# A top-p search on rows with a long tail: from bisection to a guess and a narrower search

## Chip, cores and metric

The kernel runs on one core of a Trainium2 chip. The metric is the device time of one execution in microseconds (us). The kernel before takes 1705.38 us, the median of three runs (1704.26 to 1706.78).

## The reference

Two steps of a graph layer over N = 4096 nodes with 128 features. In each step `Xa` is mixed by an attention matrix of which every row keeps only its nucleus, and `Xf` by the normalised adjacency:

```python
R = (S + eye(N)); R = R / R.sum(-1, keepdims=True)
for n in range(2):
    q = Xa @ W1.T @ W2.T;  k = Xa @ W3.T
    probs = softmax(q @ k.T)                     # (4096, 4096)
    sp = sort_descending(probs);  cs = cumsum(sp)
    keep = (cs - sp) < 0.9                       # smallest set with 90% of the mass
    A = probs * keep;  A = A / A.sum(-1)
    Xf = R @ Xf;  Xa = A @ Xa
    Z = Z + Xf @ U1[n].T + Xa @ U2[n].T
out = layernorm(x + layernorm(x + Z) * ln_g + ln_b)
```

A row's nucleus is given by one number, the weight at which it is cut. The work of the change is to find that number for the rows in which it lies deep.

## The kernel before

Each step has three stages. The **ranking** goes over the 4096 rows in 8 blocks of 512: PE computes the logits, DVE takes the eight largest of each piece with MAX8, ACT exponentiates and sums them. From the sorted largest values (24 in step one, 64 in step two) DVE finds the cut of nearly every row (`stats_step`, L1585). `norm` and `top_exp` (the smallest sorted value that counts) are written to DRAM with the cut. A row whose cut lies below what was sorted is **hard**; POOL writes its number into a list. Meanwhile PE multiplies the adjacency for `Xf` (L873).

The **search** takes the hard rows 128 at a time, one row on each partition: a tile. POOL gathers the rows of x and their `href` (the cut so far, used as the exponent's offset) and `htop` by indirect DMAs; PE computes their 4096 logits, ACT exponentiates them into a 128x4096 array of weights. DVE then looks for the cut. `tile_begin` (L2064) sets up the target, 0.9 of the total. `halve` compares all weights with a trial value, sums those above it (two passes of 2048 in step two, `part_sum` L2085; one pass of 4096 in step one, L1862), and moves the trial (`next_try`). After four of these, `chord` interpolates a trial a little below the cut, one more sum checks it (`chord_step`, `settle_chord`), then the weights below the trial are written out and summed, their eight largest per 256 taken (MAX8, L1936 and L2163), 40 of them sorted in five rounds (`sort_round`), and the cut found among these (`tile_threshold`). `hflag` says whether a row was not settled by this; PE adds the flags over partitions (L1036, L1110), and if the sum is above zero a bisection of 23 sums runs over the whole tile (inside `dve.If`), which gives the cut in any case. The new cut and norm go back to DRAM by indirect DMAs.

The **mix** goes over 8 blocks of 512 columns with 16 units each. For a unit PE computes transposed logits minus the cut into one of three psL banks (L1125, L1126), ACT exponentiates (L1450), DVE zeroes what is below 1 (`mask`, L2257), PE multiplies the result with Xa (`weigh_unit`, L1138). PE weighs unit n-3 after the logits of unit n (LAG1 = 3), and there are three buffers before and three after the mask.

In step one the mix starts when the search is over. The loop runs once on this input, but it prepares the next tile's logits at its end. In step two the list has five tiles' fetches (the last is only prepared). Tile 0 is searched ahead of the mix, with PE idle. Tiles 1 to 3 are searched between the masks of pairs of blocks: tile p+1 in pair p (blocks 2p and 2p+1). The tables `FIRST_PAIR` and `WITHIN` (L2314 on) say which step of the search stands behind the mask of which unit k = 0 to 31 of the pair. Tile p+2 is prepared in pair p: transposed at unit 8, q at unit 9 (`tile_q_lo` on DVE), its logits behind the logits of units 10 to 13, `tile_begin` at unit 14. Two of its sums above a trial are made on ACT instead (`try_piece`, L1432: per trial four Relu and four Sign passes of 128x1024, at the units of `TRIED`), and read by DVE in `summed`; the fourth trial of `halve` starts at unit 31. All engines work through their instructions in the order written, with semaphores between them. `link` puts a wait for its own instruction behind a DVE instruction.

The adjacency loads of the last two parts of step one are on SP's queue behind the first gather; POOL adds the identity to one square of them (`add_self`, L608).

## Time and profile before

| | |
|---|---|
| median of three runs | 1705.38 us |
| profiled execution | 1707.06 us |
| its span | 1704.9 us |
| PE busy | 1536.4 us (90%) |
| DVE busy | 1319.2 us (77%) |
| ACT busy | 813.6 us (48%) |
| POOL busy | 235.6 us (14%) |
| mean granted clock of PE, share of full speed | 0.948 |

A number behind L is a line of the kernel. A row of the timeline gives the start in us from the start of the span, the duration in us, the engine, the line, the operation with out<-in, and in brackets how long the engine had been idle and what released it. `DVEq` is DVE's sequencer, which handles waits and semaphores. The span has the first step up to about 760 us, the second step's ranking up to 1184, the search of tile 0 up to 1241, the mix to 1683, and then the last rows and their store.

### The profile page before, as it was taken

How to read it: one execution, taken by the hardware profiler on the slowest of the kernel's cores; microseconds unless marked ns; L12 is line 12 of the kernel's file. 1: busy time of each engine (PE TensorE's matmuls, PEld its weight loads, DVE VectorE, ACT ScalarE, POOL GpSimd, SP SyncE). 2: the span in 40 equal slices, each digit the busy share in tenths (PEclk: the TensorE clock that was granted, in tenths of full speed). 3: DMA queues.
4: the chain of work that ended last, by engine and by line, in shares of the span. 5: the costliest groups of instructions: out<-in, count | busy, mean ns of one | idle time of the engine just before them, and what ended most of it. 6: DMA issues, size and time to landing. Idle time of an engine off the chain costs nothing. (4 is left out here: it accounts for less than half of the span.)

```text
span 1704.9 us, 18073 instructions
## 1 busy us (share of the span) xinstructions
PE 1536.4 (90%) x4753; PEld 886.7 (52%) x4753; DVE 1319.2 (77%) x3739; ACT 813.6 (48%) x1301; POOL 235.6 (14%) x272
## 2 busy tenths in 40 slices
PE   7999999877999999998999999995267988988996
PEld 4555556434555555554555656653134544544553
DVE  6788888656677777776899999998968788796554
ACT  4555555312555555564444444443122836734444
POOL 2010210212000000001011111122210211311322
PEclk9999999988999999999999999997578999998998
DMA  7466666462455555555566666670000000000000
GB/s 260 173 152 151 182 190 181 109 236 96 163 187 187 188 197 203 203 203 201 184 167 171 162 195 195 196 175 1 2 3 1 1 7 7 8 1 8 7 7 13
DMA packets 53084, 211.92 MB, mean 124 GB/s; under 512 B 22096, under 2 KB 30864, under 8 KB 32512
## 3 DMA queue, kind: packets, MB, share of 16 engines
q1 hardware_dynamic: 49728, 210.59, 39.6%
q0 software_dynamic: 3264, 0.30, 0.2%
q14 instruction: 59, 0.48, 0.1%
q8 instruction: 33, 0.54, 0.1%
HBM read 206.63 MB, written 4.48 MB: 124 GB/s over the span
## 5 line engine op out<-in xcount | busy, mean ns | idle before, releaser
L1272 ACT ACTIVATE psL<-psL,umax 128x1024 f32<-128x1024 f32 x256 | 278.5, 1088 | 296.2 <-DVE umax L1755 288.3
L1761 DVE MAX8 cand<-psL 128x8 f32<-128x256 f32 (+1 forms) x640 | 371.9, 583 | 56.9 <-PE psL L904 46.9
L903 PE MATMUL psL<-kA,mq 128*128 128x512 f32 x512 | 297.5, 581 | 3.0 <-ACT psL L1272 1.6
L873 PE MATMUL psO<-adj_in,xf 128*128 128x512 f32 x512 | 241.6, 596 | 4.9 <-POOL adj_in L608 4.9
L873 PE MATMUL psO<-adj_in,xn 128*128 128x512 f32 x512 | 242.5, 597 | 3.6 <-DMA adj_in<-in_adjT 1.9
L1084 PE MATMUL psO<-ebuf,xn 128*128 128x512 f32 x512 | 241.7, 593 | 0.0
L2028 DVE SCALAR_TENSOR_TENSOR ebuf<-ebuf 128x1024 f32<-128x1024 f32 x128 | 156.7, 1225 | 99.1 <-PE psO L1084 92.6
L904 PE MATMUL psL<-kB,mq 66*128 66x512 f32 x512 | 202.5, 395 | 0.0
L1450 ACT ACTIVATE ebuf<-psL 128x1024 f32<-128x1024 f32 x128 | 129.6, 1019 | 150.6 <-PE psL L1126 109.6
L1382 ACT ACTIVATE ebuf<-psL 128x1024 f32<-128x1024 f32 x128 | 131.0, 1023 | 134.2 <-PE psL L1053 134.2
L1138 PE MATMUL psO<-xf,xa 128*128 128x512 f32 x340 | 167.0, 615 | 12.4 <-DVE xf L2257 9.4
L1125 PE MATMUL psL<-mq,kA 128*128 128x512 f32 x256 | 150.2, 587 | 13.7 <-DVEq L2250 10.4
L1052 PE MATMUL psL<-mq,kA 128*128 (+1 forms) x256 | 148.2, 579 | 3.2 <-DVEq L1995 3.2
L2257 DVE SCALAR_TENSOR_TENSOR xf<-ebuf 128x1024 f32<-128x1024 f32 x85 | 105.8, 1248 | 55.8 <-PE psO L1138 34.8
L873 PEld LDWEIGHTS psO<-adj_in,xn 128*128 128x128 f32 x512 | 96.4, 191 | 79.4 <-issue 66.6
L873 PEld LDWEIGHTS psO<-adj_in,xf 128*128 128x128 f32 x512 | 95.8, 191 | 80.2 <-issue 71.7
L1084 PEld LDWEIGHTS psO<-ebuf,xn 128*128 128x128 f32 x512 | 96.7, 190 | 74.9 <-issue 64.3
L903 PEld LDWEIGHTS psL<-kA,mq 128*128 128x128 f32 x512 | 97.1, 190 | 73.8 <-issue 45.9
L904 PEld LDWEIGHTS psL<-kB,mq 66*128 66x128 f32 x512 | 97.1, 190 | 68.6 <-issue 56.8
L1126 PE MATMUL psL<-mq,kB 66*128 66x512 f32 x256 | 104.0, 406 | 0.0
L1053 PE MATMUL psL<-mq,kB 66*128 (+1 forms) x256 | 102.5, 400 | 0.0
L1138 PEld LDWEIGHTS psO<-xf,xa 128*128 128x128 f32 x340 | 64.9, 195 | 68.4 <-issue 48.2
(366 smaller groups left out, 2051.8 us busy)
## 6 DMA issues: line engine op xcount, KB each, us to landing
adj_in<-in_adjT SPq DMA_DIRECT2D x128, 1024.0 KB
adj_in<-in_adj SPq DMA_DIRECT2D x32, 2048.0 KB, 7.7
xaT<-in_xT SPq DMA_DIRECT2D x4, 512.0 KB, 5.3
xa_dram<-xa SPq DMA_DIRECT2D x8, 256.0 KB, 7.9
out<-t SPq DMA_DIRECT2D x8, 256.0 KB
list_dram<-ids,place POOLq DMA_INDIRECT x64
rel_prob<-cut_dram SPq DMA_DIRECT2D x32, 2.0 KB
cut_dram<-ncut SPq DMA_DIRECT2D x16, 2.0 KB
```

The source lines that it names most:

```text
L873: last = nc.tensor.matmul(psO[:], fs[:, j, :], adj_in[:, r % RING, j % JQ, :], start=(j == 0), stop=(j == JT - 1))
L903: nc.tensor.matmul(o, qA[:, t * P:(t + 1) * P], kA[:, c:c + BI], start=True, stop=False)
L904: last = nc.tensor.matmul(o, qB[0:DA + 2, t * P:(t + 1) * P], kB[0:DA + 2, c:c + BI], start=False, stop=True)
L1052: nc.tensor.matmul(o, kA[:, j * P:(j + 1) * P], mqA(i), start=True, stop=False)
L1084: last = nc.tensor.matmul(psO[:], xs[:, j, :], ekept[:, u % 2, hb * BI:(hb + 1) * BI], start=(j == 0), stop=(j == JT - 1))
L1125: nc.tensor.matmul(o, kA[:, j * P:(j + 1) * P], mqA(i), start=True, stop=False)
L1138: last = nc.tensor.matmul(psO[:], xs[:, j, :], kept_unit(n)[:, hb * BI:(hb + 1) * BI], start=(j == 0), stop=(j == JT - 1))
L1272: nc.scalar.activation(ps[:], ps[:], ACT.Exp, bias=umax[:, bass.ds(i * UB + k, 1)], scale=1.0, accum_out=usum[:, bass.ds(i * UB + k, 1)]). ...
L1382: nc.scalar.activation(eraw[:, u % 2, :], psL[buffer(u, MU)][:], ACT.Exp).then_inc(g["m_exp_done"], 1)
L1450: nc.scalar.activation(raw_unit(n), psL[w % 3][:], ACT.Exp).then_inc(g["slot_read"], 1)
L1761: last = v.max(cand[:, t % 2, at + c * 8:at + c * 8 + 8], psL[(turn + k) % 3][:, c * WIDE:(c + 1) * WIDE])
L2028: v.scalar_tensor_tensor(out=ekept[:, u % 2, :], in0=eraw[:, u % 2, :], scalar=1.0, in1=eraw[:, u % 2, :], op0=ALU.is_ge, op1=ALU.mult).th ...
```

## The change

Every hard row now also takes along the sum of its sorted weights. `norm` holds one over that sum (or over the kept part of it), so a third indirect gather fetches it (`hmass`, `hmasses`), and the ranking's statistics are changed so that for a hard row `norm` has the mass of all that `top_exp` bounds. A fill of `norm_dram[1]` with ones joins two others on SP.

`guess` takes the place of the set-up in `tile_begin`: it forms the mass outside the sorted elements, what share of it is to be dropped, and from a quadratic curve a first trial that lies some elements (25 in step one, 10 in step two) below the expected cut. Step one makes no sum above a trial: it goes from the guess straight to the weights below it. Step two makes two sums of the weights below the trial (`part_sum` with `is_lt`), each followed by `narrow`, which keeps the two ends of the interval and interpolates. `halve`, `chord`, `settle_chord` and the work on ACT are gone.

Step two sorts 48 in six rounds, not 40. The eight largest are taken from every 32nd group of eight weights, not every eighth group of 32 (the `k=32` views). A row whose trial fell on the wrong side of the cut now raises its flag as well, and the bisection starts from `tupper`. The tables are new: the search of a tile has steps 0 to 11 in place of 0 to 18, and of tile p+2 both sums are made in pair p at units 22 and 27.

The diff, cut to its core (the work on ACT, the ranking's other steps and the copies for step one's other names are left out):

```diff
-    FIRST = 4
-    NEXT = 40
-    BIAS = 10.0
+    NEXTS = [40] + [48] * (STEPS - 1)
+    AHEAD_OF = [(25.0,)] + [(10.0, 10.0, 22.0)] * (STEPS - 1)
...
-                    for dst in (ref_dram, top_dram[1]):
+                    for dst in (ref_dram, top_dram[1], norm_dram[1]):
...
-                    for dst, src in ((hrefs, ref_dram), (htops, top_dram[s])):
+                        pool.wait_ge(g["cut_late"], 48 + 64 * (NB - EARLY))
...
+                        nc.gpsimd.indirect_dma_start(
+                            out=hmass[:], out_offset=None, in_=norm_dram[s],
+                            in_offset=bass.IndirectOffsetOnAxis(ap=gid[:, 1:2], axis=0),
+                            bounds_check=N - 1, oob_is_err=False).then_inc(g["h_mass"], 16)
 
                     def kept_copies(n):
 
                         pool.wait_ge(g["h_x"], n * 48 + 48)
+                        pool.wait_ge(g["h_mass"], n * 16 + 16)
                         pool.sem_inc(met, 1)
                         link(nc.gpsimd.tensor_copy(gid_out[:], gid[:]))
                         link(nc.gpsimd.tensor_copy(htop_out[:], htop[:]))
+                        link(nc.gpsimd.tensor_copy(hmass_out[:], hmass[:]))
...
-                        pool.wait_ge(g["h_ref"], r * (PT * 32) + (c + 1) * 32)
+                        fetched = c + 2 if c < PT else c + 1
+                        pool.wait_ge(g["h_ref"], r * (PT * 48) + fetched * 48)
...
+            def share(out):
+
+                link(v.scalar_tensor_tensor(out=out, in0=hthird[:], scalar=1 / 3, in1=hthird[:], op0=ALU.add, op1=ALU.mult))
+
+            def guess(st, sums, top_, mass, ref, number):
+
+                here = slice(st, st + 1)
+                link(v.tensor_reduce(ttotal[:, here], sums, AX.X, ALU.add))
+                v.tensor_scalar(ttarget[:, here], ttotal[:, here], TOP_P, None, ALU.mult)
+                v.tensor_scalar(tupper[:, here], top_, 1.0001, None, ALU.mult)
+                v.tensor_scalar(tround[:, st, 0:1], ref, 2.0 ** -22, None, ALU.mult)
+                link(v.reciprocal(hin[:], mass))
+                link(v.scalar_tensor_tensor(out=hout[:], in0=ttotal[:, here], scalar=hin[:], in1=tupper[:, here],
+                                            op0=ALU.subtract, op1=ALU.add))
+                v.tensor_scalar(tround[:, st, 1:2], tround[:, st, 0:1], -1.0, None, ALU.mult)
+                link(v.tensor_scalar(hout[:], hout[:], 1e-20, None, ALU.max))
+                v.tensor_scalar(haim[:], ttotal[:, here], 1.0 - TOP_P, None, ALU.mult)
+                v.tensor_scalar(tunit[:, here], tupper[:, here], 1.5, None, ALU.mult)
+                link(v.reciprocal(tinv[:, here], hout[:]))
+                v.tensor_tensor(tround[:, st, 0:1], tround[:, st, 0:1], tround[:, st, 1:2], ALU.max)
+                v.tensor_copy(tnumber[:, here], number)
+                link(v.tensor_scalar(tgoal[:, here], haim[:], tinv[:, here], 1.0, ALU.mult, ALU.min))
+                v.tensor_scalar(telem[:, here], tupper[:, here], tinv[:, here], None, ALU.mult)
+                link(v.tensor_scalar(hthird[:], tgoal[:, here], 2 / 3, None, ALU.mult))
+                link(v.scalar_tensor_tensor(out=hguess[:], in0=hthird[:], scalar=1 / 3, in1=tgoal[:, here], op0=ALU.add, op1=ALU.mult))
+                v.tensor_scalar(tround[:, st, 0:1], tround[:, st, 0:1], -1.0, 1.0 - 2.0 ** -20, ALU.mult, ALU.add)
+                link(v.tensor_scalar(hguess[:], hguess[:], telem[:, here], AHEAD_OF[s][0], ALU.mult, ALU.mult))
+                link(v.tensor_tensor(hguess[:], hguess[:], tgoal[:, here], ALU.add))
+                link(v.tensor_scalar(hthird[:], hguess[:], 1.0, 2 / 3, ALU.min, ALU.mult))
+                share(tnow[:, st, 0:1])
+                link(v.tensor_scalar(ttry[:, here], tnow[:, st, 0:1], tunit[:, here], None, ALU.mult))
+
+            def narrow(st, e):
+
+                here, now = slice(st, st + 1), tnow[:, st, :]
+                link(v.scalar_tensor_tensor(out=haim[:], in0=hpart[:, 0:1], scalar=hpart[:, 1:2], in1=tinv[:, here],
+                                            op0=ALU.add, op1=ALU.mult))
+                v.tensor_scalar(hin[:], haim[:], tgoal[:, here], None, ALU.is_ge)
+                link(v.tensor_scalar(hthird[:], haim[:], 1.0, 2 / 3, ALU.min, ALU.mult))
+                v.tensor_scalar(hout[:], haim[:], tgoal[:, here], None if e > 0 else 2 / 3, *((ALU.is_lt,) if e > 0 else (ALU.is_lt, ALU.mult)))
+                share(tnow[:, st, 1:2])
+                if e == 0:
+                    v.tensor_scalar(thigh[:, st, :], now, hin[:], hout[:], ALU.mult, ALU.add)
+                    link(v.tensor_scalar(tlow[:, st, :], now, hout[:], 1.5, ALU.mult, ALU.mult))
+                else:
+                    v.tensor_tensor(hfrom[:], now, thigh[:, st, :], ALU.subtract)
+                    link(v.tensor_tensor(hto[:], now, tlow[:, st, :], ALU.subtract))
+                    v.scalar_tensor_tensor(out=thigh[:, st, :], in0=hfrom[:], scalar=hin[:], in1=thigh[:, st, :], op0=ALU.mult, op1=ALU.add)
+                    link(v.scalar_tensor_tensor(out=tlow[:, st, :], in0=hto[:], scalar=hout[:], in1=tlow[:, st, :], op0=ALU.mult, op1=ALU.add))
+                v.tensor_scalar(haim[:], telem[:, here], thigh[:, st, 0:1], 1.5 * AHEAD_OF[s][e + 1], ALU.mult, ALU.mult)
+                link(v.tensor_tensor(hspan[:], thigh[:, st, :], tlow[:, st, :], ALU.subtract))
+                v.tensor_tensor(haim[:], haim[:], tgoal[:, here], ALU.add)
+                link(v.tensor_scalar(hslope[:], hspan[:, 1:2], 1e-12, None, ALU.max))
+                v.tensor_scalar(hthird[:], haim[:], 1.0, 2 / 3, ALU.min, ALU.mult)
+                link(v.reciprocal(hslope[:], hslope[:]))
+                share(hguess[:])
+                link(v.tensor_scalar(hguess[:], hguess[:], tlow[:, st, 1:2], hslope[:], ALU.subtract, ALU.mult))
+                link(v.tensor_scalar(hguess[:], hguess[:], 1.0, hspan[:, 0:1], ALU.min, ALU.mult))
+                v.tensor_tensor(tnow[:, st, 0:1], hguess[:], tlow[:, st, 0:1], ALU.add)
+                link(v.scalar_tensor_tensor(out=ttry[:, here], in0=hguess[:], scalar=tlow[:, st, 0:1], in1=tunit[:, here],
+                                            op0=ALU.add, op1=ALU.mult))
...
                     if n == 0:
+                        return v.scalar_tensor_tensor(out=ncut[:, bass.ds(i * TB, TB)], in0=half[:], scalar=0.5, in1=mx[:],
+                                                      op0=ALU.mult, op1=ALU.subtract)
+                    if n == 1:
                         dve.wait_ge(g["st_ehalf"], i + 1)
-                        return v.scalar_tensor_tensor(out=half[:], in0=hard[:], scalar=-1.0, in1=half[:], op0=ALU.add, op1=ALU.mult)
-                    if n == 1:
-                        return v.tensor_tensor(ncut[:, bass.ds(i * TB, TB)], half[:], mx[:], ALU.subtract)
+                        return v.tensor_tensor(norm[:, bass.ds(i * TB, TB)], ehalf[:], kept[:], ALU.mult)
...
-                        for k in range(1, FIRST + 1):
-                            halve(weights, rest, k)
-                        chord()
-                        above(weights, rest)
-                        settle_chord()
+                        guess(0, hsum[:, bass.ds(turn, 1), :].rearrange("p o u -> p (o u)"), htop_out[:], hmass_out[:], href_out[:], gid_out[:, 0:1])
                         below(weights, rest)
...
+                        link(v.scalar_tensor_tensor(out=hflag[:], in0=htarget2[:], scalar=0.0, in1=hflag[:],
+                                                    op0=ALU.is_le, op1=ALU.max))
+                        v.scalar_tensor_tensor(out=hflag[:], in0=tnumber[:, 0:1], scalar=float(N), in1=hflag[:],
                                                op0=ALU.is_lt, op1=ALU.mult).then_inc(g["h_flag"], 1)
...
-                        if n < 2 * FIRST:
-                            halve(c, 1 + n // 2, n % 2)
+                        if n < 4:
+                            part_sum(c, n % 2, ALU.is_lt)
+                            if n % 2 == 1:
+                                narrow(tile_slot(c), n // 2)
+                        if n in (4, 6):
+                            part_sum(c, (n - 4) // 2, ALU.is_lt)
+                        if n in (5, 7):
+                            part_largest((n - 5) // 2)
                         if n == 8:
-                            chord(c)
-                        if n in (9, 10):
-                            chord_step(c, n - 9)
-                        if n in (11, 13):
-                            part_sum(c, (n - 11) // 2, ALU.is_lt)
-                        if n in (12, 14):
-                            part_largest((n - 12) // 2)
-                        if n == 15:
                             tile_sort(c)
                             for m in range(3):
                                 sort_round(m)
-                        if n == 16:
+                        if n == 9:
                             for m in range(3, NEXT // 8):
                                 sort_round(m)
-                        if n == 17:
+                        if n == 10:
                             tile_threshold(c)
-                        if n == 18:
+                        if n == 11:
                             tile_settle(r, c)
 
-                    FIRST_PAIR = {k: k for k in range(18)}
-                    FIRST_PAIR[19] = 18
-                    WITHIN = {0: 5, 1: 6, 3: 7, 4: 8, 5: 9, 6: 10, 9: 11, 10: 12, 12: 13, 14: 14, 16: 15, 17: 16, 18: 17, 19: 18}
-                    BEGIN_AT, SUMMED_AT, FOURTH_AT = 14, (21, 30), 31
+                    FIRST_PAIR = {0: 0, 2: 1, 4: 2, 6: 3, 8: 4, 9: 5, 11: 6, 12: 7, 14: 8, 16: 9, 18: 10, 19: 11}
+                    ONE_AHEAD = {22: 0, 27: 1}
+                    WITHIN = {0: 2, 2: 3, 5: 4, 6: 5, 8: 6, 10: 7, 13: 8, 15: 9, 17: 10, 19: 11}
+                    BEGIN_AT = 14
...
-                                if k in SUMMED_AT:
-                                    summed(r, p + 2, 1 + SUMMED_AT.index(k))
-                                if k == FOURTH_AT:
-                                    search_step(r, p + 2, 4)
+                                if k in ONE_AHEAD:
+                                    search_step(r, p + 2, ONE_AHEAD[k])
...
-                    for n in range(19):
+                    for n in range(12):
                         search_step(0, 0, n)
-                        if n == 2:
+                        if n == 1:
                             z_rows(NB - 1, 0)
-                        if n == 5:
+                        if n == 3:
                             z_rows(NB - 1, 1)
-                        if n == 12:
+                        if n == 8:
                             tile_q_lo(0, 1)
```

## Rows read from the trace of the kernel before

**Rows 1.** The page, chain that ended last, shares of the span by line.

```profile
...
PE psO L1138 9%; DVE xf L2085 3%; PE psL L1125 2%; PE psL L1126 2%; DVE xf L2257 2%; DVE cand L2163 1%; DVE ebuf L2257 1%; ACT dropped L1432 0%; PE psT L1146 0%; ACT ebuf L1450 0%; DVE parts L2263 0%; ACT t L1466 0%; PE psT L1117 0%; DVE mq L2247 0%; DMA norm_dram<-hnorms,gids 0%
```

**Rows 2.** Busy time by stretch, blocks 0 to 6 of the mix: stretch, length, then each engine.

```profile
...
1252.60:1326.60 74.00, 55.78 (x156) 31.01 (x154) 63.75 (x122) 26.33 (x35) 0.07 (x1) 0.89 0.00 0
1326.60:1372.70 46.10, 43.13 (x131) 24.58 (x130) 34.44 (x80) 36.93 (x56) 12.33 (x11) 0.95 0.03 7
1372.70:1435.10 62.40, 54.42 (x167) 31.38 (x166) 52.85 (x111) 26.00 (x39) 11.90 (x10) 0.95 0.01 1
1435.10:1486.80 51.70, 45.51 (x139) 25.90 (x138) 37.07 (x95) 40.07 (x61) 12.93 (x9) 0.93 0.04 11
1486.80:1542.30 55.50, 48.15 (x139) 25.10 (x137) 51.29 (x99) 19.86 (x26) 10.19 (x7) 0.97 0.01 3
1542.30:1594.10 51.80, 45.93 (x134) 26.26 (x135) 32.82 (x80) 22.95 (x31) 13.40 (x10) 0.90 0.02 4
1594.10:1638.30 44.20, 44.20 (x139) 25.41 (x139) 26.47 (x41) 20.47 (x27) 14.06 (x10) 1.00 0.03 7
```

**Rows 3.** Timeline of DVE, search of step one.

```profile
...
361.52 4.49 DVE L1862 SCALAR_TENSOR_TENSOR ebuf<-xa,htry 128x4096 f32<-128x4096 f32 x1
...
366.75 4.49 DVE L1862 SCALAR_TENSOR_TENSOR ebuf<-xa,htry 128x4096 f32<-128x4096 f32 x1
...
406.56 0.28 DVE L1836 TENSOR_TENSOR mq<-psT,mq 64x128 fp32r<-64x128 f32 x1
...
407.62 0.16 DVE L1968 CAST hflags<-psT 128x1 int32<-128x1 f32 x1 [0.52 <-DVEq L1534]
```

**Rows 4.** Timeline of PE, the same stretch.

```profile
...
373.66 27.63 PE L873 MATMUL psO<-adj_in,xn 128*128 128x512 f32 x64
...
404.00 0.33 PE L1004 MATMUL psT<-ident,xg 128*128 128x128 f32 x1 [1.31 <-DMA htop<-top_dram,gid]
...
406.89 0.59 PE L1036 MATMUL psT<-hflag,ones 128*128 128x1 f32 x2 [1.73 <-DVE mq L1836]
```

**Rows 5.** Timeline of POOL, the two additions of the identity in that stretch.

```profile
...
359.39 1.68 POOL L608 TENSOR_TENSOR adj_in<-adj_in,ident 128x128 f32<-128x128 f32 x4 [9.01 <-DMA adj_in<-in_adjT]
392.68 3.69 POOL L608 TENSOR_TENSOR adj_in<-adj_in,ident 128x128 f32<-128x128 f32 x4 [31.61 <-DMA adj_in<-in_adjT]
```

**Rows 6.** Timeline of DVE, search of tile 0 in step two.

```profile
...
1184.38 0.16 DVE L2068 TENSOR_REDUCE ttotal<-hsum 128x1 f32<-128x4 f32 x1 [0.17 <-DVEq L1534]
...
1185.77 2.35 DVE L2085 SCALAR_TENSOR_TENSOR xf<-adj_in,ttry 128x2048 f32<-128x2048 f32 x1
...
1218.65 2.35 DVE L2085 SCALAR_TENSOR_TENSOR xf<-adj_in,ttry 128x2048 f32<-128x2048 f32 x1
...
1236.70 0.16 DVE L2215 CAST hflags<-psT 128x1 int32<-128x1 f32 x1 [0.34 <-DVEq L1534]
...
1247.93 0.42 DVE L2246 CAST cuth<-rel_prob 2x512 fp32r<-2x512 f32 x1 [3.86 <-DMA cum_keep<-cut_dram]
```

**Rows 7.** Timeline of PE, the same stretch.

```profile
...
1224.22 0.77 PE L960 MATMUL psL<-kA,hq 128*128 128x512 f32 x1 [16.01 <-DVE hq L1736]
...
1229.70 0.39 PE L961 MATMUL psL<-kB,hq 66*128 66x512 f32 x1
1235.97 0.59 PE L1110 MATMUL psT<-hflag,ones 128*128 128x1 f32 x2 [5.88 <-DVEq L2201]
```

**Rows 8.** Timeline of DVE, block 0 of the mix.

```profile
...
1285.70 1.23 DVE L2257 SCALAR_TENSOR_TENSOR xf<-ebuf 128x1024 f32<-128x1024 f32 x1 [0.22 <-DVE ttry L2107]
...
1289.68 1.23 DVE L2257 SCALAR_TENSOR_TENSOR ebuf<-ebuf 128x1024 f32<-128x1024 f32 x1 [0.22 <-DVE ttry L2142]
...
1296.74 1.22 DVE L2257 SCALAR_TENSOR_TENSOR xf<-ebuf 128x1024 f32<-128x1024 f32 x1 [3.38 <-PE psO L1138]
...
1322.36 1.23 DVE L2257 SCALAR_TENSOR_TENSOR ebuf<-ebuf 128x1024 f32<-128x1024 f32 x1 [1.94 <-ACT ebuf L1450]
```

**Rows 9.** Groups by line and shape, DVE, 1240 to 1600 us: busy us, mean ns.

```profile
...
L2163 DVE MAX8 cand<-xf 128x8 f32<-128x256 f32 x48 | 16.2, 408 | 0.0
```

More of the change, by code:

```diff
@@ L84, in gnn_kernel @@
     LOWEST = -1e30
+    LEAST = 1e-30
     PAIRS = NB // 2
@@ L317, in step_sems @@
             if s == 0:
-                names += ["h_l", "h_exp", "h_done", "m_l_ps", "m_exp_done"]
+                names += ["h_l", "h_exp", "h_done", "h_mass", "m_l_ps", "m_exp_done"]
                 names += ["r_n_ps", "r_n_sb", "m_n_ps", "m_y_sb", "m_yt_ps", "m_yt_sb", "xa_out"]
@@ L577, in _ @@
             link(nc.gpsimd.memset(htops[:], 1.0))
+            link(nc.gpsimd.memset(hmass[:], 1.0))
+            link(nc.gpsimd.memset(hmasses[:], 1.0))
             for p in range(PAIRS):
@@ L1261, in stats_half @@
                     nc.scalar.activation(top_exp[:, i * TB:(i + 1) * TB], top_rel[:], ACT.Exp)
-                    nc.scalar.activation(ehalf[:], half[:], ACT.Exp).then_inc(g["st_ehalf"], 1)
+                    nc.scalar.activation(ehalf[:], half[:], ACT.Exp, scale=-0.5).then_inc(g["st_ehalf"], 1)
                 def rank_block(i, prev, more, turn):
@@ L1652, in cut_step @@
                     if n == 14:
-                        return v.tensor_tensor(keep[:], rel[:], bc(low[:], TOP), ALU.is_ge)
+                        return v.tensor_tensor(keep[:], rel[:], bc(top_rel[:], TOP), ALU.is_ge)
                     if n == 15:
```

247 lines of the change are left out of this document (59 added, 188 removed).

## The prediction

> **What bounds the kernel now.** I read the page's chain first. The reader is to see that it follows the mix of step two: PE's weighing (L1138) leads it, and DVE's sums above a trial (L2085) come second with 3% of the span, ahead of the masks [rows 1]. Then the stretches of the mix, block by block. Block 6, in which nothing is searched, takes 44.2 us with PE busy throughout; that is the floor. Blocks 0 to 5 take 74.0, 46.1, 62.4, 51.7, 55.5 and 51.8, together 341.5, where six floors are 265. In blocks 0, 2 and 4 DVE is busy for 63.8, 52.9 and 51.3 us, more than PE has work for; there DVE sets the pace, and in block 1 it is busy for 34.4 of 46.1 and does not [rows 2]. Third, DVE's timelines of the two searches that stand ahead of a mix. In step one the search begins at 361.5, but its flag is read at 407.62 [rows 3], and PE is busy with the adjacency until 401.3 (373.66 + 27.63) [rows 4]: this search is nearly hidden. In step two tile 0 is searched from 1184.38 to 1236.70 with nothing beside it [rows 6]; PE has only the next tile's logits there [rows 7].
>
> **Step one.** Four halvings, the chord and its check go, five sums at 5.23 us each (366.75 - 361.52) [rows 3]. The search then ends near 383, and that gains almost nothing, since PE reaches the flag only after the adjacency. What is left is the order on DVE: `prepare` stood behind the search and ran at 406.56, a microsecond after q was there. Now DVE waits for it, so q's low part is done at 405.8 and not 406.84: 1.0 gained [rows 3]. What is late next is POOL's gather, which landed at 404.0; PE had been idle for 1.31 us by then, of which ACT's copy of its last transposes explains about 0.7 and the gather 0.6 [rows 4]. It was issued behind an addition of the identity that took 3.69 us beside DVE's search; the same work took 1.68 with DVE idle [rows 5]. DVE will be idle, so the gather comes 2 us earlier and PE starts at 403.4: 0.6 more. The third gather is behind the two that PE waits for and ends (some 1.3 us later) before POOL needs it; the copy of `hmass` costs 0.2 on the way to `h_done`. One instruction less in the tail of each ranking gives 0.2 in each step. SP's fill stands behind its last load, under 40 us of adjacency work, so nothing; uncovered it would be 0.4. Together -1.0 - 0.6 + 0.2 - 0.2 = -1.6, bounds 0 and -3.
>
> On the addition of the identity, the Trainium skill (SBUF — State Buffer, Who interferes with whom) says that a DVE instruction with two SBUF inputs and a GpSimd instruction that reads SBUF take one port in turn, and the second waits. By that rule 3.69 becomes 1.68; without it the gather stays late and the sum would be 0.6 smaller.
>
> **Tile 0 of step two, exposed.** From the set-up to the first sum below the trial it now takes 34.3 us (1218.65 - 1184.38) [rows 6]. After the change: the guess, two sums of two passes, two `narrow`, and the two `z_rows` (1.1 us) that stay. A pass is 2.35 and 2.4 with the read of the accumulator [rows 6]: 9.6. The trace does not have the new chains of small instructions. The nearest is the chord, 15 instructions, 11 of them linked: between two masks 3.98 us apart it takes 2.8 (mask 1.14 to the next start) [rows 8], some 0.24 per linked one. The guess has 13 linked (3.4 with its operands that are pointers), `narrow` 11 and 12 (3.3 and 3.5). As bounds I take 0.16, the busy time of one [rows 6], and 0.35 per linked one. Sum 3.4 + 9.6 + 6.8 + 1.1 = 20.9, so 13.4 less. Against it: a sixth round of sorting (0.7), 48 in place of 40 elements and one more flag instruction (0.3). DVE's flag is then ready at 1223.6. But PE has tile 1's logits in front of the flag. They wait for `tile_q_lo`, which DVE issues behind the first three rounds, at about 1218.5, and took 5.9 us with PE at its lower clock (1224.22 to 1230.1) [rows 7]. PE comes to the flag at 1224.8, not 1235.97. So the gain is 11.2, not 12.4. Everything behind it (value load, hcut, scatter, loads of the cut) moves as one. The guess for tile 1 is 2 us longer than its set-up, but DVE waited 3.86 us for the cut behind it [rows 6]: hidden.
>
> On the small instructions, the Trainium skill (VectorE: DVE Perf Modes, The TRN2 errata) has a table by which a DVE instruction on SBUF costs 58 cycles plus its elements at 0.96 GHz, 61 ns for one element. The trace has 160 ns [rows 6], and I go by that; by the page's figure the new chains would be a third as long and the whole change some 15 us better.
>
> **The mix.** Sums above or below a trial fall from 28 passes to 18, each 2.5 us between masks. I take the blocks one by one; all of it is DVE time, which counts in full where DVE sets the pace.
> - Block 0: 12 passes become 6 (-15.4), four `next_try` (-3.6), chord (-2.8), settling (-0.9); two `narrow` (+6.8), longer guess (+2.0). The mask that waited 1.94 for ACT, whose next exponential stood behind a try waiting for the set-up, doesn't wait now [rows 8]. The stall of 3.38 at unit 10 stays: PE's tile logits wait for `tile_q_lo` of a DVE that is late. Masks that stand alone pay a handshake each, +1. Net -15, 59 us.
> - Block 1: both sums of tile 2 come in, at units 6 and 11. One pass and one `narrow` more, and a slot of 9.3 us with `cut_rows`, against 3 us of `summed` that go. DVE has 11.7 us of room [rows 2], but the slot is longer than the three buffers cover (about 7 us): +2.
> - Block 2: three passes go (-7.6), tails and chord (-5.5), the wait for ACT (-1.9); one `narrow` (+3.5), guess (+2.0), six rounds of sorting moved in (+5.0): -4.5.
> - Block 3: those rounds are gone from it (-4.3), `summed` (-3), a pass and a `narrow` come (+5.9) where there is room: -3.
> - Blocks 4 and 5: as 2 and 3 without a guess or a tile ahead: -4.6 and -3.5.
> Sum -28.6. ACT loses some 38 us of tries, none of which was on the path beyond the waits named. POOL's third gather per tile (1.3 us) lies 30 us ahead of its use. At the end the set-up of a fifth tile is 2 us longer, behind which only the last store is waited for, and that is longer: nothing.
>
> MAX8 now reads groups of eight 32 groups apart. The trace shows only groups of 32, at 408 ns each as recorded, 0.34 apart [rows 9]. Per tile that is 5.4 us. I take no change; if it took twice as long, 5 us more in each of the four tiles of step two.
>
> **The sum.** -1.6 - 0.2 (step two's ranking) - 11.2 - 28.6 = -41.6 on the profiled execution's 1707.1 (span 1704.9 and 2.2 around it), 1665.5. That execution is 1.7 above the median of the runs, so 1663.8.
>
> **Rivals.**
> 1. *The guess misses (ends slower).* Step one makes no sum to check it: for each of up to 128 rows the trial must lie between 0 and 40 elements below the cut, 25 being aimed at. One row outside, or eight of the wanted ones in one of the 16 groups, raises the flag, and the bisection runs: 23 sums of 5.2 and one more, 125 us, at 407 where nothing covers it. 1663.8 + 125 = 1789. From the first such row it decides. In step two two sums correct the guess and 48 are sorted, so it is less likely; it would cost 135 per tile. For it: 128 rows with one curve for all. Against: one tile of at most 128 among 4096 rows lies past the 24 sorted, so most lie not far past them, and 15 to 25 elements is then a wide margin. No row of the trace bears on it, so the chance is a judgement.
> 2. *The bursts eat the gain.* Slots of 7 to 9 us among masks of 1.14 exceed the buffers; PE stands, and the idle slots behind cannot give it back. If blocks 1, 3 and 5 gain nothing and 0, 2 and 4 half, the mix gives 12: 1680.
> 3. *The mix goes to PE's floor.* If blocks 2 to 5 come within 2 us of 44 to 48, the mix gives 45: 1647.
> 4. *It is hidden anyway*, the loss of sums being taken up by the narrows, as DVE's sum of small instructions grows by 28 us. Then only tile 0 counts, 1694. Against: rows 2, DVE-bound blocks.
>
> **Chances.** The forecast 0.72, rival 1 0.12, rival 2 0.08, rival 3 0.06, rival 4 0.02. The range 1645 to 1683 holds the forecast with its bounds and rivals 2 and 3. 0.2% (3.4 us) is about what a measurement can tell from no change: faster 0.87, same 0.01, slower 0.12.
>
> **What would show it.** Step one: PE's flag at about 405, one sum of 4.49 in the search, no bisection. Tile 0: the flag is read near 1223.5 (1225.5 less the earlier gain), with PE's logits just before it. The mix: block 0 near 59, block 2 near 58, block 4 near 51, blocks 1, 3, 5 near 48; L2085 has 18 passes there. 400 to 408 ns for MAX8. Wrong would be a dozen or more sums of 4.49 in step one, or blocks 0, 2 and 4 above 65, 60 and 54.

## The result, and the profile after

The changed kernel takes 1677.52 us (median of 4 runs, 1671.42 to 1678.37) beside 1705.95 for the kernel before on the same chip: ratio 0.9827, interval 0.9802 to 0.9852. That is 28.4 us less, where 41.6 were forecast. The direction was right, and so was the mechanism for tile 0 and for blocks 0, 2 and 4. The mix gave 18 us and not 28.6: blocks 1 and 3 came out 12.5 us worse than forecast, and block 5 gave 4.8 of that back. The profiled execution took 1678.12 us (span 1676.3, before 1704.9).

The chain on the page still follows PE's weighing through the mix (L1148 is before's L1138); the sums above or below a trial (L2085 before, L2067 after) fell from 3% to 2%:

```profile
...
PE psO L1148 8%; PE psL L1135 2%; PE psL L1136 2%; DVE xf L2067 2%; DVE xf L2174 1%; DVE ebuf L2174 1%; DVE cand L2079 1%; ACT ebuf L1441 0%; PE psL L970 0%; PE psT L1156 0%; PE psL L971 0%; DVE parts L2180 0%; DVE cand L2094 0%; POOL rstd 
```

Busy time by stretch, blocks 0 to 6 of the mix, in the columns of [rows 2] (length, then PE, weight load, DVE, ACT, POOL, granted clock, DMA):

```profile
...
1241.60:1301.98 60.38, 51.14 (x151) 29.86 (x149) 51.25 (x123) 22.90 (x28) 1.78 (x2) 0.91 0.00 1
1301.98:1358.17 56.19, 48.11 (x133) 27.02 (x134) 39.62 (x92) 22.53 (x29) 14.46 (x10) 0.88 0.01 1
1358.17:1417.80 59.63, 54.86 (x171) 31.63 (x169) 50.67 (x129) 27.57 (x38) 17.18 (x11) 0.97 0.03 10
1417.80:1470.94 53.14, 46.49 (x130) 26.22 (x129) 38.06 (x85) 21.51 (x28) 14.85 (x9) 0.87 0.01 1
1470.94:1521.46 50.52, 47.87 (x147) 26.63 (x146) 47.05 (x106) 21.30 (x27) 9.50 (x7) 1.00 0.04 11
1521.46:1564.99 43.53, 42.51 (x134) 24.26 (x134) 29.56 (x63) 22.72 (x30) 14.06 (x10) 1.00 0.01 2
1564.99:1609.21 44.22, 44.22 (x139) 25.43 (x139) 26.47 (x41) 20.67 (x27) 15.06 (x11) 1.00 0.02 7
```

Beside [rows 2]: block 0 fell by 13.6, 2 by 2.8, 4 by 5.0, 5 by 8.3; block 1 rose by 10.1 and block 3 by 1.4. In blocks 1 and 3 DVE is busy for 39.6 of 56.2 and 38.1 of 53.1 us, so neither engine fills them, and the granted clock is at its lowest of the mix. Block 7 begins at 1609.21, before at 1638.30: 29.1, all of the gain.

Groups of DVE from 1240 to 1600 us, where before there were 28 of these sums at 2345 ns:

```profile
...
L2067 DVE SCALAR_TENSOR_TENSOR xf<-adj_in,ttry 128x2048 f32<-128x2048 f32 x18 | 44.2, 2458 | 0.0
L2079 DVE MAX8 cand<-xf 128x8 f32<-128x256 f32 x48 | 16.2, 407 | 0.0
```

Timelines of DVE, then PE and POOL, in step one; they answer to [rows 3 to 5]:

```profile
...
361.21 0.16 DVE L1534 TENSOR_REDUCE ttotal<-hsum 128x1 f32 x1 [8.32 <-ACT xa L1368]
...
364.64 4.49 DVE L1898 SCALAR_TENSOR_TENSOR ebuf<-xa,ttry 128x4096 f32<-128x4096 f32 x1
...
380.92 0.16 DVE L1955 SCALAR_TENSOR_TENSOR hflag<-tnumber,hflag 128x1 f32<-128x1 f32 x1
405.75 0.28 DVE L1885 TENSOR_TENSOR mq<-psT,mq 64x128 fp32r<-64x128 f32 x1 [24.66 <-ACT mq L1360]
```

```profile
...
374.34 27.63 PE L883 MATMUL psO<-adj_in,xn 128*128 128x512 f32 x64
...
404.24 0.32 PE L1014 MATMUL psT<-ident,xg 128*128 128x128 f32 x1 [0.88 <-ACT xf L1237]
```

```profile
...
393.21 1.69 POOL L610 TENSOR_TENSOR adj_in<-adj_in,ident 128x128 f32<-128x128 f32 x4 [31.21 <-DMA adj_in<-in_adjT]
```

One sum, no bisection; q's low part at 405.75 (406.56 before); PE waits for ACT's copy and no longer for the gather. Tile 0 of step two, DVE and then PE, beside [rows 6, 7]:

```profile
...
1183.24 0.16 DVE L1534 TENSOR_REDUCE ttotal<-hsum 128x1 f32<-128x4 f32 x1 [0.17 <-DVEq L1522]
...
1205.13 2.34 DVE L2067 SCALAR_TENSOR_TENSOR xf<-adj_in,ttry 128x2048 f32<-128x2048 f32 x1
...
1223.09 0.16 DVE L2116 SCALAR_TENSOR_TENSOR hflag<-tnumber,hflag 128x1 f32<-128x1 f32 x1
...
1225.89 0.16 DVE L2132 CAST hflags<-psT 128x1 int32<-128x1 f32 x1 [2.13 <-DVEq L1522]
1229.79 0.16 DVE L2150 RECIPROCAL hkept<-hkept 128x1 f32<-128x1 f32 x1 [3.75 <-remote]
```

```profile
...
1218.66 0.77 PE L970 MATMUL psL<-kA,hq 128*128 128x512 f32 x1 [10.08 <-DVE hq L1785]
...
1225.47 0.28 PE L1120 MATMUL psT<-hflag,ones 128*128 128x1 f32 x2
```

And block 1, the two places at which PE stands longest, PE first, then DVE's work behind unit 11. A slot is the time from the start of one unit's mask to the start of the next:

```profile
...
1310.50 0.50 PE L1120 MATMUL psT<-hflag,ones 128*128 128x1 f32 x2 [3.67 <-DVEq L2118]
...
1350.37 3.78 PE L1148 MATMUL psO<-xf,xa 128*128 128x512 f32 x4 [4.28 <-DVE xf L2174]
...
1355.37 1.88 PE L1148 MATMUL psO<-xf,xa 128*128 128x512 f32 x4
```

```profile
...
1337.72 1.51 DVE L2174 SCALAR_TENSOR_TENSOR ebuf<-ebuf 128x1024 f32<-128x1024 f32 x1 [2.77 <-ACT ebuf L1441]
1339.16 3.35 DVE L2067 SCALAR_TENSOR_TENSOR xf<-adj_in,ttry 128x2048 f32<-128x2048 f32 x1
...
1342.56 1.11 DVE L1562 SCALAR_TENSOR_TENSOR haim<-hpart,tinv 128x1 f32<-128x1 f32 x1
...
1346.78 0.68 DVE L2156 TENSOR_TENSOR mq<-psT,mq 64x512 fp32r<-64x512 f32 x1
...
1349.09 2.36 DVE L2174 SCALAR_TENSOR_TENSOR xf<-ebuf 128x1024 f32<-128x1024 f32 x2 [0.41 <-DVE mq L2164]
```

From the mask at 1337.72 to the next at 1349.09 are 11.4 us: this is the long slot. PE runs out of masked units, stands for 4.28, and what follows runs at 1.2 GHz: four weighing matmuls take 3.78 us there and 1.88 five us later. In the kernel before, the longest stop of blocks 1 and 3 was another one, early in block 3, and ACT ended it:

```profile
...
1443.05 3.78 PE L1138 MATMUL psO<-ebuf,xa 128*128 128x512 f32 x4 [6.19 <-ACT oT L1454]
...
```

ACT was at work there on the tries that the change removes. After the change no stop of PE over 0.9 us in these blocks ends with ACT. That the tries made it late is not shown by a run.

### The profile page after: what moved, and what is told of

It reads as the page before. It is cut to its first block and busy times, and to the rows that moved or that the text cites. A ratio compares the mean times of both kernels' runs of the same rounds, so it can differ in the third digit from the quotient of the medians.

```text
span 1676.3 us, 17981 instructions
## 1 busy us (share of the span) xinstructions
PE 1535.3 (92%) x4753; PEld 889.1 (53%) x4753; DVE 1267.7 (76%) x3735; ACT 779.8 (47%) x1237; POOL 245.6 (15%) x283
## 5 line engine op out<-in xcount | busy, mean ns | idle before, releaser
L1148 PE MATMUL psO<-xf,xa 128*128 128x512 f32 x340 | 167.9, 617 | 5.8 <-DVE xf L2174 5.6
L1135 PE MATMUL psL<-mq,kA 128*128 128x512 f32 x256 | 152.9, 597 | 11.2 <-DVEq L2167 11.2
L1148 PEld LDWEIGHTS psO<-xf,xa 128*128 128x128 f32 x340 | 66.5, 198 | 60.6 <-issue 45.4
```

The lines of the kernel that those rows point to most:

```text
L1135: nc.tensor.matmul(o, kA[:, j * P:(j + 1) * P], mqA(i), start=True, stop=False)
L1148: last = nc.tensor.matmul(psO[:], xs[:, j, :], kept_unit(n)[:, hb * BI:(hb + 1) * BI], start=(j == 0), stop=(j == JT - 1))
```

## The experiments

All edits are on the changed kernel. The kernel before was timed again beside each group of experiments (e1 to e4, e5 to e8, e9 to e11, e12), and its median lay between 1705.95 and 1708.94 us. So each ratio is to the kernel before as timed beside it; the changed kernel's is 0.9827. Four experiments leave the mix as it is (e4, e7, e8 and e9). With the changed kernel they show how far an unchanged mix varies: blocks 0 to 5 take 323.4 us in the changed kernel and 320.9, 323.3, 324.6 and 320.0 in the four, block 1 54.4 to 56.2, block 3 50.8 to 53.1. Part of that is the granted clock behind one and the same stop: PE stands for 3.7 us at the flag of block 1 in all of them, and over the 8 us behind it the clock is 0.57 in the changed kernel and 0.79 in e7 and e9.

**e1, the long slot.**

```diff
-                    ONE_AHEAD = {22: 0, 27: 1}
+                    ONE_AHEAD = {22: 0, 30: 1}
```

> Edit: in blocks 1 and 3 the second sum ahead and its narrow stand behind unit 14 (k = 30), not behind unit 11, where q's low part and cut_rows stand too. Theory A (one slot is too long): the slot of 11.4 us falls to about 4.2, PE's idle time of 4.28 us behind it goes in both blocks with the stretch at the lower clock that follows it; blocks 1 and 3 fall from 56.2 and 53.1 us to about 50 and 48, the time by 8 to 12 us, to about 1667. Theory B (only the sum of DVE's work in a block counts, wherever it stands): the blocks stay within 1 us, the time within 2 us of the changed kernel. Theory C: unit 14 is as bad a place, since normed_spread stands behind unit 13 and block 2's burst comes after; then 0 to 4 us.

1670.55 us, ratio 0.9776 (0.9758 to 0.9794), 7 us below e4, which was timed beside it. Blocks 1 and 3:

```profile
...
1300.91:1353.51 52.60, 48.21 (x140) 27.32 (x140) 38.82 (x93) 23.44 (x30) 14.77 (x12) 0.94 0.02 6
...
1413.12:1462.69 49.57, 46.64 (x137) 26.46 (x135) 37.27 (x85) 22.41 (x29) 12.90 (x9) 0.93 0.03 7
```

Theory A, somewhat smaller: PE stands nowhere for as much as 0.9 us behind unit 11, with nearly the same work for DVE (38.8 and 37.3 us busy, for 39.6 and 38.1). POOL's last addition of a block's rows also fell from 3.20 us beside the sum to 1.33, and the sum from 3.35 to 2.34.

**e2, the flag.**

```diff
-                            if u == 3 and i % 2 == 1 and p < PT:
+                            if u == 4 and i % 2 == 1 and p < PT:
```

with ACT's `tile_cut` at u = 5 and DVE's settling (step 11) at k = 20.

> Edit: in odd blocks PE's flag matmul stands one unit later (u = 4), DVE's settling and ACT's logarithm of the cut too. Theory A: PE's idle time at the flag (3.67 us in block 1, 2.20 in block 3, 1.02 in block 5) is the lateness of a DVE whose threshold stands behind unit 1 or 2; one unit later DVE has caught up and 3 to 6 us go, mostly in block 1. Theory B: PE would only wait for the mask in place of the flag, since the same DVE is late for both; then within 1.5 us of the changed kernel.

1670.27 us (1669.34 to 1676.41), ratio 0.9780 (0.9758 to 0.9802), so the time alone says little. PE in block 1:

```profile
...
1314.74 0.38 PE L1120 MATMUL psT<-hflag,ones 128*128 128x1 f32 x2 [1.01 <-DVEq L2118]
1351.66 3.78 PE L1148 MATMUL psO<-xf,xa 128*128 128x512 f32 x4 [6.96 <-DVE xf L2174]
```

The wait at the flag fell from 3.67 to 1.01, and the one at the long slot rose from 4.28 to 6.96 by the same 2.7 us: a PE that is earlier stands longer where DVE is late. Blocks 0 to 5 took 316.2, 4 to 8 below an unchanged mix, and block 1 53.2, 1 to 3 below. Both theories hold in part.

**e3, nothing ahead.**

```diff
-                    ONE_AHEAD = {22: 0, 27: 1}
+                    ONE_AHEAD = {}
...
-                                within = FIRST_PAIR if p == 0 else WITHIN
+                                within = FIRST_PAIR
```

> Edit: nothing is summed ahead in blocks 1 and 3; tiles 2 and 3 are searched within blocks 2 and 4 from their first sum on, in the places that tile 1 has in block 0. Theory A (DVE sets the pace in even blocks, a long slot in odd ones): blocks 1 and 3 lose the first sum, the long slot and its stalls, 56.2 and 53.1 become about 48 and 45, while blocks 2 and 4 take two sums and two narrows more (about 16 us of DVE) and become like block 0 and worse, about 68 and 60; sum +2 to +6 us. Theory B (bursts cost nothing, work counts): +12 to +16 us.

1681.30 us, ratio 0.9840 (0.9822 to 0.9858). Blocks 1 to 4, then block 5's flag on PE:

```profile
...
1300.32:1350.16 49.84, 46.05 (x134) 26.37 (x135) 31.12 (x70) 22.78 (x30) 13.10 (x10) 0.93 0.01 1
1350.16:1413.58 63.42, 52.56 (x164) 30.52 (x163) 55.44 (x145) 26.21 (x37) 18.70 (x11) 0.95 0.03 9
1413.58:1460.18 46.60, 44.34 (x134) 25.47 (x135) 31.04 (x70) 22.61 (x30) 13.40 (x9) 0.96 0.01 1
1460.18:1518.60 58.42, 51.58 (x145) 28.07 (x144) 54.55 (x121) 20.65 (x27) 11.32 (x7) 0.91 0.02 6
```

```profile
...
1527.11 0.41 PE L1120 MATMUL psT<-hflag,ones 128*128 128x1 f32 x2 [3.66 <-DVEq L2118]
```

Theory A. In block 1 the two sums ahead cost 4.6 to 6.4 us, not the 2 net that I had for them; moving them into blocks 2 and 4 costs 2 to 4 and 8 there. Block 5 takes 48.2 for 43.5, which theory A had left out: part of tile 3's sorting now falls into it (DVE busy for 31.1 us, not 29.6), and PE stands at its flag for 3.66 and not 1.02. What is left of block 1's excess, 49.8 over 46.1, is not the sums ahead.

**e4, step one's search made longer.**

```diff
                         below(weights, rest)
+                        for extra in range(4):
+                            below(weights, rest)
```

> Edit: step one's search makes four sums below the trial more, whose results are not used, 20.8 us of DVE in front of the sort. Theory A (step one's search lies under PE's adjacency, which ends at 401): the flag comes at 401.8 in place of 380.9, PE's flag matmul still near 406 and q's low part at 405.8; only POOL's addition of the identity is slowed again (3.7 us in place of 1.7) and the gather behind it comes later by 2 us, so the first mask of step one comes 0.3 to 0.8 us later. Theory B: the sums removed were part of the gain; then up to 20 us later.

1677.60 us, ratio 0.9821 (0.9800 to 0.9842): nothing. DVE, then POOL:

```profile
...
362.17 0.16 DVE L1534 TENSOR_REDUCE ttotal<-hsum 128x1 f32 x1 [8.32 <-ACT xa L1368]
...
406.74 0.28 DVE L1885 TENSOR_TENSOR mq<-psT,mq 64x128 fp32r<-64x128 f32 x1 [6.47 <-ACT mq L1360]
```

```profile
...
394.24 1.69 POOL L610 TENSOR_TENSOR adj_in<-adj_in,ident 128x128 f32<-128x128 f32 x4 [31.17 <-DMA adj_in<-in_adjT]
```

From the search's start to q's low part are 44.57 us here and 44.54 in the changed kernel: step one's search is hidden to 0.1 us. Not even the 0.3 to 0.8 came, since POOL's addition fell beside the sorting and not beside a sum, and took 1.69.

**e5, no code to jump over.** A flagged tile would not be repaired.

```diff
-                        with dve.If(unsettled > 0):
-                            fresh_chain()
-                            link(v.tensor_scalar(ttry[:, st:st + 1], tupper[:, st:st + 1], factor[1] / factor[0], None, ALU.mult))
...
```

> Edit: the code of the bisection in step two's settling, which no tile enters, is left out (so a flagged tile would not be repaired). Theory A (the wait of 3.70 to 3.75 us between the copy of the flags and the reciprocal, in tiles 0 to 2, is DVE fetching instructions beyond code that it jumps over): the wait falls to under 1.5 us everywhere. Tile 0's settling gives 2.2 us on the path to the cut, blocks 1 and 3 up to 2.2 each; 3 to 6 us less than the changed kernel. Theory B (it is the wait for PE's flag, or the register's load): the waits stay at 3.7 and the time within 1 us.

1672.09 us, ratio 0.9790 (0.9777 to 0.9803). Settling of tile 0:

```profile
...
1224.67 0.16 DVE L2132 CAST hflags<-psT 128x1 int32<-128x1 f32 x1 [2.21 <-DVEq L1522]
1225.77 0.16 DVE L2137 RECIPROCAL hkept<-hkept 128x1 f32<-128x1 f32 x1 [0.94 <-DVE hflags L2132]
```

3.75 us became 0.94: the wait is DVE's and hangs on the code of 24 sums that it jumps over. What DVE does in that time no run shows. Of the 2.8 us in tile 0, 1.3 arrive at the mix (57.0 from tile 0's guess to the first mask, not 58.4); ACT's fourth exponential of tile 1 and the load of its table for the logarithm stood in front of that. In the mix the shorter wait alone shows little: block 1 takes 54.5 and block 3 49.8, beside 54.4 to 56.2 and 50.8 to 53.1, and PE stands as long as before at the flag and behind the long slot (3.67 and 4.28). The rest of the gain in time can't be told from how the profiled executions vary.

**e6, the edits of e1 and e2 together.**

> Edit: both moves at once, the second sum ahead behind unit 14 and PE's flag with its followers one unit later. Theory A: with the later flag alone, PE's idle time at the long slot grew from 4.28 to 7 us, so the long slot took back what the flag gave. Without it the two gains add: blocks 1 and 3 near 49.5 and 47.8 us (56.2 and 53.1 changed kernel), block 5 near 41, the time 12 to 15 us below the changed kernel and about 5 below the kernel with the moved sum alone. Theory B: DVE's work in the odd blocks is the limit by then, the later flag gives nothing beyond the moved sum: 8 to 9 us below the changed kernel.

1665.81 us, ratio 0.9744 (0.9731 to 0.9757). Blocks 1 and 3:

```profile
...
1303.18:1352.79 49.61, 45.51 (x140) 25.34 (x140) 38.66 (x93) 23.12 (x30) 15.47 (x12) 1.00 0.03 7
...
1412.40:1460.17 47.77, 44.00 (x137) 24.48 (x135) 37.06 (x84) 22.05 (x29) 13.56 (x9) 1.00 0.03 7
```

Theory A: 49.6 and 47.8 as expected, the clock at 1.00 in both, blocks 0 to 5 at 310.0. Blocks 1 and 3 together are 4.8 below e1's; the later flag alone (e2) had brought 0.9 to 4.8 there, since the long slot took part of it back.

**e7 and e8, the guess missing.** In e8 the number is 10.

```diff
-    AHEAD_OF = [(25.0,)] + [(10.0, 10.0, 22.0)] * (STEPS - 1)
+    AHEAD_OF = [(80.0,)] + [(10.0, 10.0, 22.0)] * (STEPS - 1)
```

> Edit: step one's guess aims 80 elements below the cut where 40 are sorted, so that the sorted ones do not reach the cut and the bisection runs. It prices the rival that the guess misses. By the prediction 24 sums of 5.2 us, 125 us, at a place where nothing covers them: 1802 us. If something covered part of it (or one flagged row cost less), clearly below 1790.

> Edit: step one's guess aims 10 elements below the cut in place of 25. By the prediction's reason against the rival (the rows lie not far past the 24 sorted, a margin of 15 to 25 elements is wide) the margin has room, but one row of 128 too low is enough: if no row is off by more than 10 elements, the time stays at 1677; if one is, it is 1802. I hold the second for somewhat likelier (0.6).

At 80, 1676.48 us (one run): no bisection, so my reading of the number as elements that must stay under 40 was wrong. At 10, 1798.67 us (one run), and the bisection runs:

```profile
...
408.81 0.15 DVE L1965 TENSOR_SCALAR ttry<-tupper 128x1 f32<-128x1 f32 x1 [0.88 <-DVE hflags L1961]
...
528.78 0.16 DVE L1972 RECIPROCAL hkept<-hkept 128x1 f32<-128x1 f32 x1 [0.37 <-DVE hkept L1969]
```

120.0 us for 24 sums, 5.0 each, all of it in the time. Rival 1's price stands (125 forecast), and on the low side the 25 is less than a factor of 2.5 from the number at which the guess misses. This holds for the one input measured.

**e9, tile 0's flag first.**

```diff
                         tile_logits(0, 1, n, (NU + n) % 3)
-                    tile_flag(0, 0)
+                        if n == 2:
+                            tile_flag(0, 0)
```

> Edit: in front of the mix PE computes tile 0's flag behind the third unit of tile 1's logits in place of behind the fourth and last. Theory A (by the prediction, what PE has in front of the flag costs 1.2 us; the trace after shows DVE's flag at 1223.25 and PE's matmul at 1225.47): the flag comes 1.5 us earlier, and with it settling, scatter, the loads of the cut and the whole mix: 1.2 to 1.7 us less than the changed kernel. Theory B: what counts behind it is ACT, whose fourth exponential of tile 1 (to 1226.9) stands in front of the logarithm, or the loads: 0 to 0.5. The mix's start in the trace, relative to the guess of tile 0, tells it, the time alone does not.

1673.74 us, ratio 0.9799 (0.9784 to 0.9814). PE's flag is 1.6 us earlier and is read 1.4 earlier, counted from tile 0's guess; the first mask is 0.9 earlier (57.5 for 58.4). Between A and B: ACT stands in front of the rest.

**e10, narrow apart.** The same is done for `ONE_AHEAD` and tile 0.

```diff
-                            if n % 2 == 1:
-                                narrow(tile_slot(c), n // 2)
...
+                                if within.get(k - 1) in (1, 3):
+                                    narrow(tile_slot(p + 1), within[k - 1] // 2)
```

> Edit: each narrow stands behind the unit after its sum's, alone, in blocks 0 to 4; the amount of work is the same. Theory A (where DVE has more to do in a block than PE, the block's sum of work counts and not its slots; where it has room, the longest slot counts): blocks 0, 2 and 4 within 1 us of 60.4, 59.6 and 50.5; the slot at unit 11 of blocks 1 and 3 falls from 11.4 to 7.5 us and gives 2 to 3 us in each: time -4 to -6. Theory B (every slot of 7 us makes PE stand, in even blocks too): blocks 0, 2 and 4 also fall by 2 us or more each, time -10 or more.

1801.09 us, and that is my mistake: in front of the mix the edit narrowed tile 0 with the numbers of the other slot, so its sorted elements missed the cut and the bisection ran (flags read at 1223.88, reciprocal at 1355.92: 132 us, rival 1 said 135). The mix itself is as meant. Blocks 0 to 3:

```profile
...
1367.97:1429.19 61.22, 50.90 (x151) 29.56 (x149) 51.26 (x123) 22.90 (x28) 1.78 (x2) 0.90 0.00 1
1429.19:1483.06 53.87, 48.08 (x143) 26.84 (x144) 38.81 (x92) 22.65 (x30) 15.23 (x10) 0.97 0.01 2
1483.06:1542.87 59.81, 53.05 (x160) 30.16 (x158) 50.06 (x130) 26.89 (x38) 17.01 (x11) 0.94 0.04 10
1542.87:1593.19 50.32, 44.83 (x140) 25.15 (x139) 37.04 (x85) 21.36 (x29) 14.27 (x9) 1.00 0.01 1
```

Even blocks don't care how their work is cut up (block 4 took 50.69). The odd ones lie 0.5 below the shortest of an unchanged mix, so the 2 to 3 us did not come. PE's stop behind the slot fell from 4.28 to 1.65, but the slot is 7.4 and the next is 4.6: two long slots in a row count nearly like one.

**e11, all moves.** The edits of e6 and e9, and:

```diff
-                            for k in range(1, FINE + 1):
+                            with dve.Fori(0, FINE) as k:
+                                fresh_chain()
                                 whole_sum(c)
...
-                                link(v.tensor_scalar(hstep[:], habove[:], ttarget[:, st:st + 1], up - up / factor[k], ALU.is_ge, ALU.mult))
+                                link(v.tensor_scalar(hstep[:], habove[:], ttarget[:, st:st + 1], rise[:, bass.ds(k, 1)], ALU.is_ge, ALU.mult))
```

> Edit: the second sum ahead behind unit 14, PE's flag and its followers one unit later, the flag of tile 0 behind the third unit of tile 1's logits, and step two's bisection as a loop of 23 turns with its factors in a small table, so that the code which DVE jumps over is short. Theory A: the moves of the two slots give 14 us, the short code what leaving it out gave (6 us, of it 2.2 before the mix), the early flag 1.2: near 1658 to 1660, the settling's wait at 0.9 to 1.5 us. Theory B: with DVE no longer late in the odd blocks the short code gives only what stands before the mix, near 1663. If the wait stays at 3.7 us, a loop's code is fetched as slowly as 23 copies of it.

1665.69 us, ratio 0.9754 (0.9741 to 0.9768), no better than e6. The short code did its part: the wait in tile 0's settling is 1.17, and blocks 1 and 3 take 47.6 and 45.6, 2.1 less each than in e6. With the other two waits mended it counts; in e5 it hardly did. But 46 small fills had gone into GpSimd's set-up, and PE's first projection came at 12.99 us:

```profile
...
12.99 3.44 PE L830 MATMUL psL<-xaT,wk 128*128 128x512 f32 x4 [7.57 <-POOLq L599]
```

**e12, the mended version.**

```diff
             dve.sem_inc(stored, 16)
+            for k in range(1, FINE + 1):
+                here = math.exp(SPAN / 2 ** k)
+                up = here if k == FINE else math.exp(SPAN / 2 ** (k + 1))
+                v.memset(rise[:, k - 1:k], up - up / here)
+                last = v.memset(fall[:, k - 1:k], up / here)
+            link(last)
             dve.wait_ge(ready, 2)
...
-                        tile_exp(0, 1, n, (NU + n) % 3, NU + n + 1)
-                    tile_cut(0, 0)
+                        if n == NU - 1:
+                            tile_cut(0, 0)
+                        tile_exp(0, 1, n, (NU + n) % 3, NU + n + 1)
```

> Edit: the kernel with all moves, with two mends. Its 46 small fills of the factor table leave GpSimd's set-up, which PE and DVE wait for (PE's first projection began at 12.99 us there, at 7.47 in the changed kernel, and its first logits at 23.12 in place of 19.15), and stand on DVE in front of its first wait, where it is idle for 5.7 us. And ACT takes the logarithm of tile 0's cut in front of the fourth exponential of tile 1, behind which it stood (hmid ready near 1229.2, logarithm at 1232.25). Theory A: 4.0 us from the set-up and 1.5 from the cut, 5.5 less than the kernel with all moves: near 1660, a ratio of about 0.972 to the kernel before. Theory B: the set-up's delay is taken up before the mix by a wait that both kernels have, as POOL's or the loads' in step one; then only the cut's 1 to 1.5 us.

1659.43 us (1658.18 to 1662.14), ratio 0.9717 (0.9704 to 0.9731): 48 us below the kernel before and, by the two ratios, about 19 below the changed one. By the two ratios it is 6 us below e11, as in theory A. The two profiled executions do not show where: tile 0's guess is at 1185.86 for 1186.69, though PE started 5.4 earlier, and only 1.2 more come from there to the first mask. Blocks 1 and 3:

```profile
...
1303.52:1351.05 47.53, 45.25 (x140) 25.45 (x140) 38.63 (x93) 23.34 (x30) 14.54 (x12) 1.00 0.03 7
...
1410.65:1456.24 45.59, 43.66 (x137) 24.59 (x135) 37.05 (x84) 22.31 (x29) 12.67 (x9) 1.00 0.03 7
```

No run entered the loop of the bisection in step two, so neither its speed nor that it repairs a flagged tile is shown.

## Why the prediction was right or wrong

The forecast's -41.6 on the profiled execution came out as -28.9.

**Step one, -1.6: the causes right, the sum in part by luck.** The first mask stands at 421.90 and not 423.52, 1.6 earlier. But PE's adjacency work, which hides the search, ended 0.7 later (374.34 + 27.63, before 373.66 + 27.63). Counted from its end, q's low part came 1.5 earlier, for 1.6 from the two causes named, and the first mask 2.3 earlier. The other 0.8, between q and the mask, I had not forecast and can't explain. (The forecast's 405.8 is the end of q's low part; its row begins at 405.75 and ends at 406.03.) The identity's addition took 1.69 for 3.69. That agrees with the rule quoted from the Trainium skill (SBUF — State Buffer, Who interferes with whom), and e1's POOL row (3.20 and 1.33) repeats it. Tile 0's guess comes at 1183.24, 1.1 ahead of 1184.38, but over the runs with the same code up to there it lies anywhere from 1181.45 (e3) to 1187.49 (e2). So a forecast of 1.8 ahead of tile 0 can't be tested on that row.

**Tile 0, -11.2: direction right, 1.4 too large.** From the guess to the first pass that also writes out the weights below the trial are 21.9 us, 20.9 forecast. The guess took 4.07 us for 3.4, with one small instruction of 0.76 in it, and the first pass 2.53; the two `narrow` took 3.24 and 3.77 for 3.3 and 3.5. The term for PE's logits was too small: 6.8 us for 5.9. The 5.9 had been read as wholly at the lower clock, but before the change the last third of these matmuls took 0.40 us and not 0.63 each (granted clock 0.64 over 1224.22 to 1230.10); after it they ran at the lower level nearly throughout (0.52). The flag came at 1225.47, 2.2 behind DVE's. The first mask is 11.0 earlier, with 1.1 of it from ahead of tile 0: 9.8 (58.4 us from the guess, before 68.2).

**Blocks 0, 2, 4: right.** 60.4, 59.6 and 50.5 against 59, 58 and 51. Where DVE has more to do than PE the sum of its work is what counts; e3 and e10 show it from both sides.

**Blocks 1 and 3: the steps that failed.** "+2" was 8 to 10, and "-3" was between -0.9 and +1.4. (Block 3's own terms, -4.3 - 3 + 5.9, add up to -1.4; the -3 took part of what came in as hidden, without saying how much.)

I had seen the danger ("the slot is longer than the three buffers cover") and sized it by the sum of work. Three things were missing. First, the slot is 11.4 us and not 9.3, since it falls beside POOL's additions, which slow the sum and the first small instruction behind it by 1.9. Second, behind the stops of 3.67 and 4.28 us PE runs its next units at 1.2 GHz; the granted clock of block 1 fell from 0.95 to 0.88. Third, PE's wait for the flag at unit 3 is new: DVE, later in block 1 than before, has the threshold, the settling and a jump of 3.7 us in a row (before, 1.5 in this block). The forecast for this block has neither the jump nor a PE that holds logits back behind the flag.

Step by step, block 1 goes from 54.4 to 56.2 down to 52.6 with the sum moved (e1), 49.6 with the later flag (e6) and 47.5 with the short code (with the changes of e11 and e12), and block 3 from 50.8 to 53.1 down to 49.6, 47.8 and 45.6. The end is near the forecast's 48 and 49, though for a kernel with other places for this work. 

One more term was wrong, the other way: of ACT's tries "none was on the path beyond the waits named", but PE stood for 6.19 us in block 3 before and ACT ended it, and that stop is gone. It hides part of the miss in block 3.

**Block 5, -3.5: it gave 8.3.** Before, PE stood at its flag for 5.75 us, now for 1.02; the forecast had only DVE's work. Whether the shorter block 4 or the sorting moved out of block 5 makes the flag early, no run separates; e3, which takes back some of both, has 3.66 and a block of 48.2. **MAX8: right,** 407 ns with groups 32 apart. **The end:** nothing, as forecast.

**Rivals.** The measured 1677.52 lies 2.5 us from rival 2's 1680 and 13.7 from the forecast. Rival 2 named the mechanism of blocks 1 and 3 (slots longer than the buffers cover) and was too mild there; in the even blocks and in block 5 it was wrong, so its time is close by two errors that cancel. Rival 1's price was measured (120 and 132 us), and the guess held; rivals 3 and 4 are out. My time was low mostly because I took the even blocks' rule, work counts, for blocks 1 and 3, where long slots and late hand-overs count.

## What to carry to other kernels

Ask of each stretch whether the engine is short of time or only late. Short: count its work, and its order doesn't matter. With room: count the longest stretch between two hand-overs (here, from one mask to the next) against what the buffers cover, take stretches that follow each other together (e10), and place long work away from other work that slows it. After removing one wait look where the partner stands next (in e2 PE's wait at one place fell by 2.7 us and rose by 2.7 at another), and mend both before judging either. A mend that shows little alone can count once the others are made: the short code gave block 1 nothing clear in e5 and 2.1 us on top of e6.

## What the hardware showed beyond that

- Where DVE jumps over the large body of step two that is not entered, 3.7 to 4.05 us pass until its next instruction, in some passes less (in the changed kernel tiles 0 to 2 had 3.7, tile 3 1.45; before, only tiles 0 and 2 had it; in e4 tile 1 had 1.87). With the body left out it is 0.90 to 1.25, with the body as a loop 1.12 to 1.46. Why passes differ is open.
- Two-input DVE sums and POOL additions slow each other: 3.35 for 2.34 us, and 3.20 for 1.33. Beside DVE's sorting POOL's addition kept its 1.69.
- 46 fills of one column on POOL took some 7 us of set-up, while DVE made them in its idle time at the start without moving PE's first projection (7.59 us beside 7.47).
